# A three-layer interaction kernel: its program written out chunk by chunk, with other kinds for its couples, a ring for the spread fields, a first layer loaded in parts, and the last two chunks' layers interleaved

## The reference

```python
x0 = xk = inputs                                   # (512, 39, 16)
for idx, (W, b) in enumerate([(w0, b0), (w1, b1), (w2, b2)]):
    z = jnp.einsum('bhd,bkd,hks->bsd', x0, xk, W) + b[None, :, None]
    z = jax.nn.relu(z)                             # (512, 128, 16)
    if idx != 2:
        xk = z[:, :64, :]                          # the maps of the next layer
        direct.append(z[:, 64:, :])
    else:
        direct.append(z)
logit = jnp.sum(jnp.concatenate(direct, axis=1), axis=-1)   # (512, 256)
```

## Time and profile before

| | value |
|---|---|
| median of 3 runs | 597.0 us (594.65 to 597.07) |
| the profiled execution's own time | 594.9 us |
| its span | 593.1 us |
| PE busy | 569.8 us (96%) |
| DVE busy | 509.5 us (86%) |
| POOL busy | 453.4 us (76%) |
| ACT busy | 339.8 us (57%) |
| mean granted clock of TensorE | 0.994 |

### The profile page before, as it was taken

The page is one execution under the profiler, slowest core; times in us unless marked ns, Lnnn a source line. Parts: engine busy times, 40 slices in busy tenths (PEclk is TensorE's granted clock), DMA queues, the critical chain, the costliest instruction groups (busy, mean ns, idle before and its releaser), DMA issues.

```text
span 593.1 us, 7442 instructions
## 1 busy us (share of the span) xinstructions
PE 569.8 (96%) x1952; PEld 370.0 (62%) x1952; DVE 509.5 (86%) x471; ACT 339.8 (57%) x372; POOL 453.4 (76%) x196
## 2 busy tenths in 40 slices
PE   2699999999999999999999999999999999999977
PEld 0366666666666666666666666766666666666644
DVE  2789999898889989888998989989898998988853
ACT  1556567474755747576474656647465574747542
POOL 0268969698796969969696896969779696987965
PEclk9999999999999999999999999999999999999989
DMA  8939985380926629083571918448092653900000
GB/s 311 421 138 371 421 331 225 143 353 5 369 120 236 259 105 384 6 335 160 204 291 59 385 50 291 204 167 328 22 384 88 253 242 133 362 1 0 1 2 35
DMA packets 17406, 121.55 MB, mean 205 GB/s; under 512 B 2058, under 2 KB 2058, under 8 KB 5108
## 3 DMA queue, kind: packets, MB, share of 16 engines
q1 hardware_dynamic: 16992, 120.59, 52.0%
q10 hardware_dynamic: 404, 0.84, 0.5%
HBM read 120.90 MB, written 0.52 MB: 205 GB/s over the span
## 4 chain that ended last, share of the span: by engine, by line
PE 95%; DMA 2%; ACT 1%; DVE 1%; issue 0%; ACTq 0%
PE z L435 95%; DMA field_spread<-w0s 2%; ACT hi L478 1%; DVE raw L259 0%; ACT maps L493 0%; DVE d_raw L259 0%; DVE sums L305 0%; ACT z L501 0%; ACTq L526 0%; DVE field_spread L341 0%; ACTq L536 0%
## 5 line engine op out<-in xcount | busy, mean ns | idle before, releaser
L370 POOL TENSOR_TENSOR lo<-raw,hi 128x1024 fp32r<-128x1024 f32 x192 | 453.2, 2394 | 134.2 <-ACT hi L478 119.6
L478 ACT ACTIVATE hi<-raw 128x1024 fp32r<-128x1024 f32 x192 | 203.2, 1059 | 123.0 <-DVE raw L259 118.2
L435 PE MATMUL z<-exact,w_exact 128*128 128x512 f32 (+2 forms) x544 | 260.1, 603 | 10.3 <-DVE exact L259 10.3
L259 DVE TENSOR_TENSOR raw<-field_spread,maps 128x1024 f32<-128x1024 f32 x192 | 228.2, 1217 | 27.4 <-ACT maps L493 27.4
L435 PE MATMUL z<-hi,w_hi 128*128 128x512 f32 (+1 forms) x480 | 209.8, 437 | 9.1 <-ACT hi L478 9.1
L435 PE MATMUL z<-hi,w_lo 128*128 128x512 f32 (+1 forms) x448 | 178.0, 397 | 0.0
L435 PE MATMUL z<-lo,w_hi 128*128 128x512 f32 (+1 forms) x480 | 177.6, 462 | 0.0
L435 PEld LDWEIGHTS z<-exact,w_exact 128*128 128x128 f32 (+2 forms) x544 | 104.7, 193 | 93.8 <-issue 71.6
L435 PEld LDWEIGHTS z<-lo,w_hi 128*128 128x128 f32 (+1 forms) x480 | 90.4, 188 | 53.0 <-issue 38.1
L435 PEld LDWEIGHTS z<-hi,w_hi 128*128 128x128 f32 (+1 forms) x480 | 90.6, 189 | 42.5 <-issue 19.6
L259 DVE TENSOR_TENSOR exact<-field_spread,maps 128x1024 f32<-128x1024 f32 x96 | 116.7, 1216 | 0.0
(11 more groups left out here) (11 smaller groups left out, 22.4 us busy)
## 6 DMA issues: line engine op xcount, KB each, us to landing
field_spread<-x_spread SPq DMA_DIRECT2D x80, 1024.0 KB, 7.6
fields<-x_fields SPq DMA_DIRECT2D x16, 1280.0 KB, 7.1
fields<-x_fields SPq DMA_DIRECT2D x16, 768.0 KB, 4.5
field_spread<-w1s SPq DMA_DIRECT2D x1, 896.0 KB, 12.8
field_spread<-w2s SPq DMA_DIRECT2D x1, 896.0 KB, 17.8
field_spread<-w0e ACTq DMA_DIRECT2D x1, 585.0 KB
out<-sums SPq DMA_DIRECT2D x2, 256.0 KB, 2.1
w_exact<-w1e SPq DMA_DIRECT2D x1, 384.0 KB, 13.3
```

The source lines that it names most:

```text
L259: nc.vector.tensor_tensor(ring, spread[0:rows, 2 * k:2 * k + tiles, :], by[0:rows, :].unsqueeze(1).to_broadcast([rows, tiles, COLS]), ALU. ...
L370: nc.gpsimd.tensor_tensor(lo[0:rows, slot % LO_RING, :, :], raw[0:rows, raw_slot % RAW_RING, :, :], hi[0:rows, slot % HI_RING, :, :].bitca ...
L435: mm = nc.tensor.matmul(z[layer][:, :], w[0:rows, :], part[0:rows, :], start=(step == 0 and p == 0), stop=(step == len(order) - 1 and p == ...
L478: nc.scalar.activation(hi[0:rows, slot % HI_RING, :, :], products, ACT.Copy).then_inc(hi_ready, 1)
```

## The change

- The kinds are `("SDEE", "SSEDSSSEDS", "SDSSSEESDS")`: 6 exact couples (11 tiles) and 18 split ones (36 tiles) in a chunk, 5 of these of kind D. Chunk 0 has its own: `("EEEE", "SSEDSSSEDS", "ESESSEESDS")`.
- The rings of raw, hi and lo have 3, 6 and 5 slots instead of 4, 5 and 3.
- There are no loops on the engines any more: each engine's program is written out for all 16 chunks, and a table gives the place of each couple in each ring.
- The spread fields are in a ring of seven groups of four tiles. A group is loaded when layer 2 is done with the one seven before; so two groups of the next chunk come before its layer 0's fields, three behind them. The last two slots first hold the staged split weights of layers 1 and 2.
- At the start layer 0's weights, their transposed half and the fields come in three parts each, in turn, all on SP's queue. DVE sums a part and multiplies its couple. In chunk 0 it multiplies by the fields' slot in SBUF, without ACT's copy. Layer 1's weights are split in two halves: w_lo of the first 8 tiles by POOL before its first `lo`, of the rest by DVE after six couples of layer 1; w_lo of layer 0 is made by POOL, w_hi of layers 0 and 2 by ACT, in round 0.
- In round 14 the last three couples of layer 2 are kept back. The order at the end is layer 1 of chunk 15, these three couples of chunk 14, layer 2 of chunk 15 (accumulated in `z[0]`). Most of the output is stored before the last chunk's sums, which follow in DMAs of their own.
- The sums stand elsewhere: of the last layer after 8 couples of layer 1 (7 before), of `direct` after 6 couples of layer 2 (8 before); ACT's `direct` alone now waits for the sum before, its two maps no longer.

```diff
-KINDS = ("EDEE", "SESSSESDES", "SESSESSDES")
+KINDS = ("SDEE", "SSEDSSSEDS", "SDSSSEESDS")
+KINDS_FIRST = ("EEEE", "SSEDSSSEDS", "ESESSEESDS")
-RAW_RING = 4
-HI_RING = 5
-LO_RING = 3
+RAW_RING = 3
+HI_RING = 6
+LO_RING = 5
+QUADS = TILES // 4
+SPREAD_RING = 7
+W0_CUTS = (0, 2, 4, TILES0)
+W1_AT = 6
+KEPT = 7
+LAST = CHUNKS - 1
+FIELD_CUTS = (0, 3, 5, 1 + TILES0)
+def segments():
+    yield 0, 0, range(COUPLES[0])
+    for c in range(LAST):
+        yield 1, c, range(COUPLES[1])
+        yield 0, c + 1, range(COUPLES[0])
+        yield 2, c, range(KEPT if c == LAST - 1 else COUPLES[2])
+    yield 1, LAST, range(COUPLES[1])
+    yield 2, LAST - 1, range(KEPT, COUPLES[2])
+    yield 2, LAST, range(COUPLES[2])
...
+            def load_spread(c, q):
+                slot, count = quad(c, q)
+                if count > 1:
+                    before, part = divmod(c * QUADS + q - SPREAD_RING, QUADS)
+                    wait_multiplied(sp, 2, before, 2 * part + 1)
...
+            for p in range(3):
+                a, e = W0_CUTS[p:p + 2]
+                sp.dma_start(w_exact[0][0:ROWS0, a:e, :], w0[:, a:e, :]).then_inc(w0_loaded[p], 16)
+                sp.dma_start(w0_transposed[0:ROWS0, a:e, :], w0t[:, a:e, :]).then_inc(w0t_loaded[p], 16)
+                load_fields(0, p)
...
-                        if slot >= RAW_RING:
+                        if count >= RAW_RING:
                             dve.wait_ge(s_lo_ready, count - RAW_RING + 1)
...
+            for k in range(3):
+                sum_weights0(k)
+                multiply(0, 0, range(k, k + 1))
+            multiply(0, 0, range(3, COUPLES[0]))
+            for c in range(LAST):
                 dve.wait_ge(z0_evacuated, 3 * c + 2)
+                if c == 0:
+                    multiply(1, 0, range(0, W1_AT))
+                    weights_split_lo(1, 8, 2)
+                    multiply(1, 0, range(W1_AT, COUPLES[1]))
...
+            for c in range(LAST):
+                if c:
                     pe.wait_ge(z1_evacuated, 3 * c)
+                contract(1, c, range(COUPLES[1]))
+                pe.wait_ge(z0_evacuated, 3 * c + 3)
+                contract(0, c + 1, range(COUPLES[0]))
...
+                contract(2, c, range(KEPT if c == LAST - 1 else COUPLES[2]))
+            pe.wait_ge(z1_evacuated, 3 * LAST)
+            contract(1, LAST, range(COUPLES[1]))
+            contract(2, LAST - 1, range(KEPT, COUPLES[2]))
+            pe.wait_ge(z0_evacuated, 3 * CHUNKS)
+            contract(2, LAST, range(COUPLES[2]))
```

More of the change, by code:

```diff
@@ L60 @@
[L60 to L90, removed]
@@ L98, in cin_kernel, with schedule @@
+def schedule(layer, c, couples):
+    todo, pending = [], []
+    for k in couples:
+        kind = kinds(layer, c)[k]
+        todo.append(("exact" if kind == E else "hi", k))
+        if kind != E:
+            pending.append(k)
+        if pending and k - pending[0] >= LO_LAG and k != couples[-1]:
+            todo.append(("lo", pending.pop(0)))
+    return todo + [("lo", k) for k in pending]
+def cin_kernel(nc, x_fields, x_spread, w0, w0t, w1e, w1s, w2e, w2s, b, out):
     fp32 = mybir.dt.float32
@@ L196, in wait_multiplied @@
[L196 to L208, removed]
@@ L259, in multiply @@
-                    nc.vector.tensor_tensor(ring, spread[0:rows, 2 * k:2 * k + tiles, :],
+                        products, ready = d_raw[0:rows, 0:tiles, :], d_raw_ready
+                    nc.vector.tensor_tensor(products, by_field,
                                             by[0:rows, :].unsqueeze(1).to_broadcast([rows, tiles, COLS]),
                                             ALU.mult).then_inc(ready, 1)
-                    if k >= D_LAG and KINDS[layer][k - D_LAG] == D:
-                        split_lo_couple(layer, place("SD", i, d, layer, k - D_LAG, more))
@@ L265, in split_lo_couple, with split_lo @@
-            def split_lo_couple(layer, counts):
-                count, slot = counts
+                    if k - D_LAG in couples and kinds(layer, c)[k - D_LAG] == D:
+                        split_lo(layer, c, k - D_LAG)
+                for k in couples[-D_LAG:]:
+                    if kinds(layer, c)[k] == D:
+                        split_lo(layer, c, k)
+            def split_lo(layer, c, k):
+                count = PLACE["SD"][layer, c, k]
                 rows = 128 if layer else ROWS0
@@ L402, in contract @@
-            def contract(layer, i, d, more=True):
-                tiles = (TILES0, TILES, TILES)[layer]
-                order = schedule(layer)
+            def contract(layer, c, couples):
+                order = schedule(layer, c, couples)
+                tiles = LAYER_TILES[layer]
                 for step, (what, k) in enumerate(order):
-                    kind = KINDS[layer][k]
-                    count, slot = place(E if kind == E else "SD", i, d, layer, k, more)
-                    m = count_kind(KINDS[layer][:k], E if kind == E else "SD")
+                    kind = kinds(layer, c)[k]
@@ L420, in contract @@
-                    e, h, l = (slot % ring for ring in (EXACT_RING, HI_RING, LO_RING))
+                        if (layer, c) == (0, 0) and k < 3:
+                            pe.wait_ge(w0_summed, k + 1)
+                    else:
+                        count = PLACE["SD"][layer, c, k]
+                        if what == "hi":
+                            pe.wait_ge(hi_ready, count + 1)
+                        else:
+                            pe.wait_ge(s_lo_ready if kind == S else d_lo_ready, PLACE[kind][layer, c, k] + 1)
@@ L476, in split_hi @@
+                    place = PLACE[kind][layer, c, k]
+                    act.wait_ge(raw_ready if kind == S else d_raw_ready, place + 1)
+                    if count >= HI_RING:
                         act.wait_ge(lo_used, count - HI_RING + 1)
-                    products = raw[0:rows, kind_slot % RAW_RING, :, :] if kind == S else d_raw[0:rows, :, :]
-                    nc.scalar.activation(hi[0:rows, slot % HI_RING, :, :], products,
+                    products = raw[0:rows, place % RAW_RING, :, :] if kind == S else d_raw[0:rows, :, :]
```

558 lines of the change are left out of this document (288 added, 270 removed).

## The result

The changed kernel takes 577.9 us (median of 4 runs, 576.82 to 578.18), the kernel before 595.8 us beside it (594.65 to 597.07). The ratio is 0.970, 95% interval 0.967 to 0.973: faster, and inside the range of 568 to 584. The profiled execution took 578.0 us with a span of 576.2; the forecast, made against the 594.9 of the profiled execution before, was 573.4. So 16.9 us were won where 21.5 were forecast.

The account below looks back on a forecast made before the run. PE was taken to bound the kernel by its work a round and its gaps. Start 3.0, rounds 1 to 13 12.3 and end 6.2 sum to 21.5 us; 594.9 less that is 573.4, stated as 574, range 568 to 584.

Parts of the forecast that it names:

- The bound and the price of a couple: Middle rounds: PE bounds them; three couples turned from exact to split save 0.315 us each, 0.945 a round, giving 34.16.
- DVE fits: Middle rounds: DVE needs 33.4 us of a 34.16 us round, keeping 0.7 for waits.
- the walk through one round: DVE and POOL timed through a middle round: PE never waits; DVE waits 0.7 us for the maps before layer 2.
- the longer ring of lo: Middle rounds: five slots instead of three remove 2.35 us of DVE's subtractions waiting for a slot PE must still read.
- The end: From layer 1 of chunk 14 on: kept couples cover the 3.84 us gap and remove half pace; 6.2 us less.
- The start: Chunk 0: layer 1 starts 5.9 us earlier, round 0 lasts 2.4 longer, late spread fields cost 0.5; net 3.0 gained.
- The landing of the first fields: Start of chunk 0: first weights and fields, 1.0 MB, land at 6.5 us, with bounds 4.7 and 7.9.
- Layer 0 on PE: Chunk 0: seven exact tiles take 8.2 us, 4.4 of them at slow pace, and are done at 15.9.
- the sum for round 0: Round 0: PE work 34.8 us, half pace 1.8, waits for weights 1.0, 1.1 and 0.6; sum 39.3.
- The tail: From DVE's last sum to the end of the span: stays as it was, a smaller store but the same wait.
- Loops and instruction supply: Whole kernel: writing loops out gains nothing and costs zero; rival of ten 2 us stops leaving 594 us, 4%.
- the fourth: Rival: the start gives nothing, PE at half pace through layer 0 and round 0 longer by weights; 577 to 578, 13%.

Follow-up runs that it names:

- Run 9: Changed kernel with layer 1's small weight instruction moved to POOL and layer 0's weights in two DMAs behind the fields' first part: 575.5 us, 0.969 of the kernel before.
- run 5: Changed kernel with the small instruction for the last tile of layer 1's w_hi moved from DVE to POOL: 575.4 us, 0.968 of the kernel before.
- the three traces with 41.9: Traces of the changed kernel, its unaltered rerun (578.6 us), and the changed kernel with no layer 2 couples kept back (582.3 us).
- run 1: Changed kernel with only the kinds undone, 9 exact and 15 split couples a chunk: 591.6 us, 0.996 of the kernel before.

## Why the prediction was right, and where it wasn't

- **The bound and the price of a couple** were right. 0.945 us a round by arithmetic, 34.16 measured, 35.09 again when undone.
- **DVE fits** was right: 0.7 us to spare in the forecast, 0.5 measured, and the walk through one round named the one place of its wait. The reason given beside it, that the longer ring of lo removes 2.35 us of waits, wasn't: three slots give 34.44. Nor does any run try the ring of raw alone, which the walk called the tightest.
- **The end** was right in size and in both halves: the gap of 3.84 and the half pace; 4.6 us when undone against 4.5 to 6.
- **The start** failed: "Net: 5.9 - 2.4 - 0.5 = 3.0 us" was -2.0, just outside its own bounds of -1 and +5. Three terms were mis-sized. The landing of the first fields was taken at 6.5, by the rate of the kernel before, and was 8.39: the queue moved 207 GB/s in the first 10 us, not 272. Run 9 has the fields at 6.36 with nothing ahead of them, so the 1.9 us go with the weights that stand ahead in the queue; 0.86 of them is the later issue (1.60 instead of 0.74). Layer 0 on PE was taken at 8.2 us with 4.4 at half pace and took 9.2, as half pace lasted 5.3 us, until 14.96, and PE had two short stops for later parts. And round 0 took 41.9, not 39.8: one instruction of 0.29 us lasted 2.05 longer under contention, and with it gone (run 5) the round takes 39.7. That term was known, put beside the sum as up to 2.4 us, and left out of it, since only the Trainium skill and no row had it. The sum with it, 576, was the nearer one: 578.0 measured in the profiled execution. The form of the sum for round 0 was wrong too: it added PE's half pace to PE's waits, and the three traces with 41.9 show that the one is taken out of the other. That the forecast 39.8 meets run 5's 39.7 is then in part luck.
- **The tail** was taken as unchanged and is 0.7 shorter.
- **Loops and instruction supply** at zero: right, by the 35.09 of run 1 and by PE's unbroken run of 502 us in the changed kernel.

Of the rivals, the fourth, that the start gives nothing, happened by its number (577 to 578; 577.9 measured). Its mechanism did so in part: round 0 was longer, but layer 0 was at half pace for 5.3 of its 9.2 us and not throughout.

## What to carry to other kernels

Where one engine is busy for the whole of a steady round, price the round by the spacing of its instructions, and then walk the other engines through one round with their rings; here this gave the round to 0.01 us. Distrust the stretches that occur once: the start had three wrong terms, and one instruction of 0.29 us cost 2. Before an instruction moves to another place in time, ask where its inputs lie and which other engine works on SBUF there; and when the ranges are cut at which a deferred step is flushed, look at what falls on the cut.

## What the runs showed of the hardware

- A VectorE product with both inputs in SBUF beside GpSimd subtractions took 3.36 us (mean of 15) instead of 1.22, an instruction of 64 x 128 elements 2.34 instead of 0.29, one of 128 x 1920 elements 4.00 instead of 2.16, and five GpSimd subtractions 13.82 instead of 11.8. The one that started first kept its time (1.22), and the other took 3.41 instead of 2.36.
- 0.84 MB of weights in six DMAs landed at 19.4 us on a second queue beside a full one (924 packets), at 13.1 in turn on one queue; in two DMAs on the second queue (404 packets, the kernel before) at 12.75.
- Behind its pause of 3.85 us TensorE went at half pace (0.43 us a pass instead of 0.23) from 572.59 to 576.55 in the kernel before, with a granted clock of 0.57 there, which is mostly its lower level, 1.2 GHz. In the kernel after it was from 22.70 to 28.78 (0.51), behind a pause of 3.87 us and a first layer that was partly at half pace too. The same kernel run again, behind the same pause, first went at full pace (0.99) and fell to half only from 24.66 to 28.60 (0.57). In layer 0 of chunk 0 the matmuls from 9.67 to 14.96 are 0.85 us apart, where full pace is 0.43, though the profile's granted clock says 1.00 there.

```profile
9.67:15.98 6.31, 6.31 (x8) 2.37 (x8) 3.35 (x5) 0.00 (x0) 0.00 (x0) 1.00 1.04 352
22.70:28.78 6.08, 6.08 (x13) 3.85 (x13) 5.61 (x5) 4.12 (x5) 5.70 (x3) 0.51 1.01 415
```
